# A cross-attention and FFN layer on one core: plain fp32 operands in place of pairs of fp32r parts in all FFN products

## The reference

```python
x = x + xattn(layernorm(x), ctx)       # 8 heads of 32, causal mask over 77 keys, softmax, projections Wq Wk Wv Wo with biases
x = x + ffn(layernorm(x))

def ffn(x):                            # weights are ternary (-1, 0, 1); s is a scale per output feature
    h = silu((x @ w1.T) * w1_s) * ((x @ w2.T) * w2_s)      # 256 -> 1024
    h = gelu((h @ h1.T) * h1_s)                            # 1024 -> 1024
    h = gelu((h @ h2.T) * h2_s)                            # 1024 -> 1024
    return (h @ w3.T) * w3_s                               # 1024 -> 256
```

## Time and profile before

| | |
|---|---|
| median of the runs | 1544.83 us |
| the profiled execution, its own time | 1543.65 us |
| its span, first to last instruction | 1541.9 us |
| PE (TensorE matmul) busy | 1532.9 us, 99% of the span |
| PEld (weight loads, beside PE) busy | 1249.0 us, 81% |
| DVE (VectorE) busy | 802.0 us, 52% |
| ACT (ScalarE) busy | 697.2 us, 45% |
| POOL (GpSimd) busy | 123.1 us, 8% |
| period of one pass of the loop | 92.78 us |

### The profile page before, as it was taken

One profiled execution on the slowest core, in us unless ns is written; L12 is line 12 of the kernel. 1 busy time (PEld: TensorE's weight loads), 2 busy tenths in 40 slices (PEclk: granted clock), 3 DMA queues, 4 the chain that ended last, 5 costly groups with the idle time before them and its releaser, 6 DMA issues.

```text
span 1541.9 us, 21318 instructions
## 1 busy us (share of the span) xinstructions
PE 1532.9 (99%) x8422; PEld 1249.0 (81%) x8422; DVE 802.0 (52%) x1276; ACT 697.2 (45%) x1013; POOL 123.1 (8%) x134
## 2 busy tenths in 40 slices
PE   9999999999999999999999999999999999999998
PEld 6787888888888887888888888887888888888887
DVE  6664735547354474644548354474644547354332
ACT  4653534436354453534536354353634536354342
POOL 1001011010100201001010100201001010100000
PEclk9999999999999999999999999999999999999999
DMA  9951020212202121020212202121030211202000
GB/s 377 347 189 50 32 84 27 75 48 65 57 14 77 53 67 49 31 85 27 75 41 64 65 14 75 55 67 49 24 92 27 75 41 64 64 16 68 14 1 15
DMA packets 50529, 106.32 MB, mean 69 GB/s; under 512 B 9026, under 2 KB 24394, under 8 KB 47690
## 3 DMA queue, kind: packets, MB, share of 16 engines
q1 hardware_dynamic: 50506, 106.00, 21.1%
HBM read 61.93 MB, written 32.52 MB: 61 GB/s over the span
## 4 chain that ended last, share of the span: by engine, by line
PE 96%; DMA 1%; SPq 1%; DVE 0%; ACT 0%; issue 0%; ACTq 0%
PE ffn_banks L479 84%; PE att_banks L660 4%; PE att_banks L602 3%; PE att_banks L619 2%; PE att_banks L650 2%; DMA h_bits<-in_h 1%; PE att_banks L670 1%; SPq L370 1%; PE ffn_banks L693 0%; ACT junk L725 0%; SPq L349 0%; PE ffn_banks L685 0%; DVE inexact L861 0%; PE att_banks L590 0%; DVE a_lo L887 0%
## 5 line engine op out<-in xcount | busy, mean ns | idle before, releaser
L479 PE MATMUL ffn_banks<-b_hi,h_sb 128*128 128x512 f32 x1024 | 404.4, 395 | 0.0
L479 PE MATMUL ffn_banks<-b_lo,h_sb 128*128 128x512 f32 x1024 | 399.0, 390 | 0.0
L479 PE MATMUL ffn_banks<-a_hi,h_sb 128*128 128x512 f32 x1024 | 398.3, 389 | 0.0
L479 PE MATMUL ffn_banks<-a_lo,h_sb 128*128 128x512 f32 x1024 | 398.3, 389 | 0.0
L759 ACT ACTIVATE a_f<-ffn_banks,vec 128x512 f32<-128x512 f32 x128 | 88.2, 689 | 367.1 <-PE ffn_banks L479 367.1
L887 DVE TENSOR_TENSOR a_lo<-a_f,a_hi 128x512 fp32r<-128x512 f32 x128 | 94.5, 739 | 298.0 <-ACT a_hi L760 297.9
L479 PEld LDWEIGHTS ffn_banks<-b_hi,h_sb 128*128 128x128 f32 x1024 | 192.3, 188 | 45.1 <-issue 6.2
L479 PEld LDWEIGHTS ffn_banks<-a_hi,h_sb 128*128 128x128 f32 x1024 | 192.2, 188 | 39.9
L479 PEld LDWEIGHTS ffn_banks<-a_lo,h_sb 128*128 128x128 f32 x1024 | 192.2, 188 | 39.9
L479 PEld LDWEIGHTS ffn_banks<-b_lo,h_sb 128*128 128x128 f32 x1024 | 192.3, 188 | 38.9
L479 PE MATMUL ffn_banks<-ln_hi,w_sb 128*128 128x512 f32 x512 | 203.6, 398 | 0.6 <-DVE v_later L915 0.6
(11 more groups left out here) (103 smaller groups left out, 1580.9 us busy)
## 6 DMA issues: line engine op xcount, KB each, us to landing
blocks_dram<-blocks SPq DMA_DIRECT2D x30, 512.0 KB, 3.0
attn_t<-blocks_dram SPq DMA_DIRECT2D x60, 256.0 KB
h_bits<-in_h SPq DMA_DIRECT2D x8, 1024.0 KB, 19.1
h_sb<-h_bits SPq DMA_DIRECT2D x8, 1024.0 KB, 8.5
out<-out_sb SPq DMA_DIRECT2D x32, 256.0 KB, 2.0
x_in<-in_x SPq DMA_DIRECT2D x15, 512.0 KB, 3.6
ln_t<-in_x_t SPq DMA_DIRECT2D x14, 512.0 KB, 4.4
ln_rows<-ln_rows_dram SPq DMA_DIRECT2D x14, 512.0 KB, 4.0
```

Source lines behind the costliest of these rows:

```text
L479: mm = nc.tensor.matmul(psum, left, right, start=(k == 0 and part == 0), stop=(k == rows - 1 and part == 1))
```

## The change

- The FFN's weights and hidden rows are plain fp32 tiles. Each FFN product is one matmul instruction in the program; `product`, `product_general`, `signal` and the parts `hi` and `lo` are gone, and with them the casts, the second Gelu and the subtractions, and the step `L1E`.
- The steps `CHECK`, `COUNT`, `FLAG`, `READ` and `KEEP`, the copies of the weights onto themselves, the ring, the general program and the branch are gone. TensorE waits for the loaded pieces themselves.
- From tile 1 on, the normalised rows are not transposed on TensorE: VectorE transposes 32x32 blocks (two instructions of 128x512), one DMA (`XW`) writes 512 KB to DRAM and four DMAs (`XR`) read them back into `ln2_t`. The tokens of a tile stand in another order in `ln2_t`; the Gelu of L3 puts them back. `T2` stays for tile 0.
- `PV` stands ahead of `L2` 7 instead of behind it, `O` behind `L3` 0 instead of `L3` 1, `LN1S` ahead of `LN2A`. SyncE's waits in `MV` and `ROWS` are other ones; buffers lie elsewhere, with their own room for `q_t`, `ln2_t` and `attn_t`.

```diff
-    ("L2", 1), ("MV", 0), ("L2", 2), ("MV", 1), ("L2", 3), ("L2", 4), ("L2", 5), ("L2", 6), ("L2", 7), ("PV", 0), ("PV", 1),
-    ("L3", 0), ("L3", 1), ("O", 0), ("CTX", 0), ("LN2S", 0), ("L3", 2), ("LN2A", 0), ("LN1S", 0), ("L3", 3), ("ROWS", 0), ("L3", 4),
-    ("L3", 5), ("LN1A", 0), ("L3", 6), ("T2", 0), ("L3", 7), ("Q", 0), ("L4", 0),
+    ("L2", 3), ("L2", 4), ("L2", 5), ("L2", 6), ("PV", 0), ("PV", 1), ("L2", 7),
+    ("L3", 0), ("O", 0), ("CTX", 0), ("LN2S", 0), ("L3", 1), ("LN1S", 0), ("LN2A", 0), ("XW", 0), ("ROWS", 0), ("XR", 0),
+    ("L3", 2), ("L3", 3), ("L3", 4), ("LN1A", 0), ("L3", 5), ("L3", 6), ("L3", 7), ("Q", 0), ("L4", 0), ("L4", 1),
...
-    ("KEEP", 0, 0), ("SPILL", 0, 0), ("KEEP", 1, 0), ("SPILL", 1, 0), ("KEEP", 2, 0),
+    ("SPILL", 0, 0), ("SPILL", 1, 0),
...
-                        if n == 0:
-                            sp.wait_ge(up_ready, KH * f + KH)
-                        else:
-                            sp.wait_ge(stored, 32 * f + 32)
+                        sp.wait_ge(stored, 32 * f + 32)
...
+                    if step == "XW":
+                        sp.wait_ge(rows_blocked, t)
+                        sp.dma_start(row_blocks_dram.rearrange("k p b i -> p k (b i)"), row_blocks[:].rearrange("p k b i -> p k (b i)"))\
+                            .then_inc(row_blocks_out, 16)
+                    if step == "XR":
+                        sp.wait_ge(row_blocks_out, 16 * t)
+                        sp.wait_ge(up_ready, KH * f + KH)
+                        for b_ in range(4):
+                            src = row_blocks_dram[:, :, b_, :].rearrange("k (r f) i -> f (k r) i", r=4)
+                            dst = ln2_t[32 * b_:32 * b_ + 32].rearrange("f k (r i) -> f (k r) i", r=4)
+                            sp.dma_start(dst, src).then_inc(ln2_there, 16)
...
-                    for part, x_ap in enumerate((hi(k), lo(k))):
-                        left, right = (x_ap, w_sb(k)) if w_is_moving else (w_sb(k), x_ap)
-                        mm = nc.tensor.matmul(psum, left, right, start=(k == 0 and part == 0),
-                                              stop=(k == rows - 1 and part == 1))
...
+                            for k in range(KD):
+                                mm = nc.tensor.matmul(fb[:, 2 * (n % 2) + i, :], w_sb[:, k, n * P:(n + 1) * P], ln2_t[:, k, :],
+                                                      start=(k == 0), stop=(k == KD - 1))
+                            mm.then_inc(ready, 1)
...
+                        for k in range(KH):
+                            if n == 0:
+                                pe.wait_ge(piece_loaded[first_piece + k // 2], 16)
+                            if n == 0 and (k == 0 or k >= at_once):
+                                pe.wait_ge(rows_done, KH * f + max(k + 1, at_once))
+                            mm = nc.tensor.matmul(fb[:, n % 4, :], w_sb[:, k, n * P:(n + 1) * P], rows[:, k, :],
+                                                  start=(k == 0), stop=(k == KH - 1))
...
+                                mm = nc.tensor.matmul(fb[:, 2 + n, i * D:(i + 1) * D], a_sb[:, k, j * P:(j + 1) * P], w3_sb[:, k, :],
+                                                      start=(k == 0), stop=(k == KH - 1))
...
-                        nc.scalar.activation(f32[:, n, :], fb[:, n % 4, :], ACT.Gelu, scale=scale[:, n:n + 1])
-                        nc.scalar.activation(hi[:, n, :], fb[:, n % 4, :], ACT.Gelu, scale=scale[:, n:n + 1]).then_inc(done, 1)
+                        if step == "L2":
+                            dst, src = rows[:, n, :], fb[:, n % 4, :]
+                        else:
+                            dst = rows[:, n, :].rearrange("p (j r q) -> p r j q", j=NQ, r=4)
+                            src = fb[:, n % 4, :].rearrange("p (r j q) -> p r j q", j=NQ, r=4)
+                        nc.scalar.activation(dst, src, ACT.Gelu, scale=scale[:, n:n + 1]).then_inc(done, 1)
...
+                            for k in range(KD):
+                                op = nc.vector.transpose(row_blocks[:, k, :, :],
+                                                         xln[:, :, k * P:(k + 1) * P].rearrange("p j (b f) -> p b j f", b=4))
+                            op.then_inc(rows_blocked, 1)
```

More of the change, by code:

```diff
@@ L141, in build_kernel @@
[L141 to L162, removed]
@@ L167, in build_kernel @@
+        put("later_rest", [P, 512])
+        c_later, _ = put("c_later", [P, KD * LATER], at=later_at)
+        v_later, _ = put("v_later", [P, NCH, D], at=later_at + 4 * KD * LATER)
+        assert later_at + 4 * KD * LATER + 4 * NCH * D <= top[0]
+        k_later, k_later_at = put("k_later", [P, HG * LATER])
+        q_t, _ = put("q_t", [P, HG, TILE])
+        ln2_t, _ = put("ln2_t", [P, KD, TILE])
+        attn_t, _ = put("attn_t", [TK, H, TQ])
         w_att_sb, _ = put("w_att_sb", [P, 4, KD, D])
@@ L295, in later_keys @@
             return k_later[:, HG * GROUP * g:HG * (GROUP * g + group_width(g))].rearrange("p (m n) -> p m n", m=HG)
[L297 to L314, removed]
         block = es.enter_context(nc.Block())
@@ L370, in load_piece, with one_pass @@
                 sp.dma_start(pieces[c][1], pieces[c][0]).then_inc(piece_loaded[c], 16)
[L372 to L390 removed]
+            def one_pass(f, a, b):
+                for step, n, t in steps(f, a, b):
                     if step == "SPILL" and n == 0:
@@ L471, in _ @@
         def _(pe):
-            def product(psum, w_sb, rows, hi, lo, ready, base_n, w_is_moving=False):
-                for k in range(rows):
-                    if ready is not None:
-                        pe.wait_ge(ready, base_n + k + 1)
-                    for part, x_ap in enumerate((hi(k), lo(k))):
-                        left, right = (x_ap, w_sb(k)) if w_is_moving else (w_sb(k), x_ap)
-                        mm = nc.tensor.matmul(psum, left, right, start=(k == 0 and part == 0),
-                                              stop=(k == rows - 1 and part == 1))
-                return mm
-            def product_general(psum, c, f, rows, hi, lo, ready, base_n, w_is_moving=False):
-                for k in range(rows):
-                    if ready is not None:
-                        pe.wait_ge(ready, base_n + k + 1)
-                    pe.wait_ge(ring_loaded[(c + k) % 2], (16 * (CHUNKS // 2)) * f + 16 * ((c + k) // 2 + 1))
-                    for part, x_ap in enumerate((hi(k).bitcast(F32), lo(k).bitcast(F32))):
-                        w_ap = ring[(c + k) % 2][:]
-                        left, right = (x_ap, w_ap) if w_is_moving else (w_ap, x_ap)
-                        mm = nc.tensor.matmul(psum, left, right, start=(k == 0 and part == 0),
-                                              stop=(k == rows - 1 and part == 1))
-                    mm.then_inc(ring_used, 1)
-                return mm
-            def signal(sem_, general):
-                if general:
-                    nc.tensor.drain().then_inc(sem_, 1)
             def spin(count):
@@ L565, in one_pass @@
-                        if general:
-                            signal(l4_ready, general)
-                        else:
-                            mm.then_inc(l4_ready, 1)
+                            for k in range(KH):
+                                if j == 0 and (k == 0 or k == KH - 1):
+                                    pe.wait_ge(gelu3_done, KH * f + max(k + 1, KH - 1))
+                                mm = nc.tensor.matmul(fb[:, 2 + n, i * D:(i + 1) * D], a_sb[:, k, j * P:(j + 1) * P], w3_sb[:, k, :],
+                                                      start=(k == 0), stop=(k == KH - 1))
@@ L663, in one_pass @@
                         mm.then_inc(o_ready, 1)
-                    if step == "T2":
+                    if step == "T2" and f is None:
                         pe.wait_ge(ln_ready[1], t + 1)
-                        if f is None:
-                            pe.wait_ge(q_done, 2)
+                        pe.wait_ge(q_done, 2)
                         for k in range(KD):
@@ L968, in one_pass @@
                         ln_apply(x1, 1, t)
-                    if step == "T2":
-                        dve.wait_ge(ln2hi_done, t + 1)
-                        nc.vector.tensor_tensor(ln2_lo[:], ab[:, 0:2, :], ln2_hi[:].bitcast(F32), ALU.subtract).then_inc(ln2t_done, 1)
+                        if f is not None:
+                            dve.wait_ge(ln_ready[1], t + 1)
+                            for k in range(KD):
+                                op = nc.vector.transpose(row_blocks[:, k, :, :],
+                                                         xln[:, :, k * P:(k + 1) * P].rearrange("p j (b f) -> p b j f", b=4))
+                            op.then_inc(rows_blocked, 1)
                     if step == "LN1S":
```

224 lines of the change are left out of this document (56 added, 168 removed), and 18 rows, old and new, of tables (FIRST, ORDER).

## The result

The changed kernel takes 2662.14 us (median of four runs, 2661.05 to 2663.31) against 1544.57 us: a ratio of 1.7234, 95% interval 1.7204 to 1.7264. The profiled execution has a span of 2659.3 us with a mean granted clock of 1.000, 1117.4 us longer than before.

The account below looks back on a forecast made before the run. TensorE bounds the kernel by what its matmuls cost back to back; 1541.9 + 1130 (FFN products) - 13 (transposes) - 3 (beginning) - 1 (a wait) = 2655 us of span, 2658 us in time, range 2635 to 2700.

Parts of the forecast that it names:

- the likeliest case: Whole kernel: the forecast itself, 2658 us, with its own range 2640 to 2675 us and chance 0.86.
- What bounds the kernel: TensorE's matmuls back to back set the time; shortening another engine's work cannot show.
- The products of L1 to L3: FFN layers L1 to L3: 320 records a tile go from 0.2267 to 0.4283 us each, adding 64.5 us a tile.
- anything but 428 ns: Sign of being wrong: plain records in L2 following one another at any distance other than 428 ns.
- L4: Last FFN layer, 256 columns: 64 records a tile go from 7.70 to 13.8 us, adding 6.1 us a tile.
- rival B: FFN's plain records carry the fp32r stream's surcharge of 13.4 ns: 72 us more, 2730 us; chance 0.06.
- rival A: L1 to L3: a long plain stream runs quicker, a product costing what a pair costs; 1528 us; chance 0.02.
- T2 and the way through DRAM: Transposes leave TensorE for tiles 1 to 15: 13 us less, the DRAM way of about 30 us hidden under 65 us.
- rival C, D: C: DRAM way exceeds its 65 us cover, 2733 us, chance 0.04. D: clock partly at 1.2 GHz, 2.9 ms, 0.02.
- ScalarE's and VectorE's relief: Casts, second Gelus and subtractions removed: some 280 us less busy time each, no gain in the kernel's time.
- The beginning: Before the loop: between 0 and 6 us can go, 3 us taken; first L1 at 62 to 67 us.

Follow-up runs that it names:

- e1_l3_plain: Kernel before with plain fp32 operands in L3 only, without its low-part subtraction and the second Gelu ahead of it; span 1956.1 us, time 1957.88 us.
- e2_t2_on_pe: Changed kernel with the normalised rows' transposes back on TensorE for every tile, no way through DRAM; span 2672.8 us, time 2674.63 us.
- e5_plain_halves: Changed kernel with each 512-column product of L1 to L3 issued as two of 256 columns; span 2672.4 us.
- e10_parts_dram_early: Kernel before with rows through DRAM, in the changed kernel's order around O and the layer norms, split into parts behind Q; 1531.09 us, ratio 0.9906.
- e3_parts_dram: Kernel before, fp32r parts kept, with normalised rows of tiles 1 to 15 transposed on VectorE and brought through DRAM; 1545.60 us, ratio 0.9999.
- e4_hi_only: Kernel before with the low parts' FFN matmuls left out, the work that makes them kept; span 1337.4 us.
- e7_late_rows: Changed kernel with the normalised rows' DRAM write and reads moved from L3 1 to behind L4 0 and its store; span 2750.0 us.
- e8_start_order: Changed kernel with the keys' and values' products before the loop back in the old kernel's places; span 2656.6 us.
- e9_grouped: Kernel before with each FFN sum's high parts all issued first, then all low parts; span 1560.0 us.
- e6_parts_halves: Kernel before with each 512-column part in L1 to L3 issued as two of 256 columns; span 1620.9 us.

## Why the prediction was right

It was right: 2658 us forecast, 2662.14 measured, inside the range of 2635 to 2700 and inside the likeliest case's own. By its steps:

- **What bounds the kernel.** Right: the chain after is TensorE's, and the experiments that changed TensorE's records moved the span by their price as long as TensorE stayed the bound (`e1_l3_plain`, `e2_t2_on_pe`, `e5_plain_halves`, `e10_parts_dram_early`; not `e3_parts_dram` and `e4_hi_only`, where another chain took over).
- **The products of L1 to L3.** 64.5 us a tile forecast, 64.6 measured. Q's short stretch spoke for the long one: 428.3 ns read there, 429.2 in the FFN. Over 5120 records the 0.9 ns are 4.6 us, mostly offset by smaller extras at the switches between steps (0.6 us a pass against 0.8), which I had held constant; that the two sums agree to 0.1 us is in part luck. Taken to the letter, my sign of being wrong ("anything but 428 ns") was drawn too narrowly. The row that foretold the pace was the one of the same kind of operand in another step, not the one of the FFN itself.
- **L4.** 6.1 us a tile forecast and measured, 215.8 ns a record against 215.6.
- **The surcharge (rival B) and the quicker stream (rival A).** Neither came: plain records keep 2.5 ns beyond their columns in long streams and in halves, parts 13 ns in both. The trace's 429.2 ns for two walks over 512 columns agrees with the columns over 2.4 GHz plus 2.5 ns that the Trainium skill gives for an isolated matmul ("TensorE: Matmul & The Clock Gate", section "Back-to-back issue gap"), taken for 1024 columns; the 226.7 ns of a part do not agree with it, being 10.9 ns above its value for 512. That section's 131 ns for 512 columns in a stream is seen in no run here, neither with plain operands nor with parts.
- **T2 and the way through DRAM.** 13 us forecast, 13.5 by `e2_t2_on_pe`. From O's end to the last reads I allowed 30 us; it took 18 (O's end at 328.4, the last reads landed at about 346.7), and `e7_late_rows` shows 7.5 us from the write's issue to L1. The argument had a gap that did not matter in the changed kernel: I followed the chain that was moved and left out the one behind it on VectorE, the next tile's statistics, which the transposes on TensorE had covered, and what the new traffic may do to that chain's DMA steps. `e3_parts_dram` shows that it takes the whole gain in the short pass. I had also priced a lost cover at 15 us for each us; with the clock it is 15 x 6.0 for 3.6 us of waiting, 1.7 times that (rival C, D).
- **ScalarE's and VectorE's relief.** Worth nothing, as forecast. The amounts were 241 and 259 us and not 280. The weight loads' share fell to 50% and not to 47%.
- **The beginning.** Wrong by 3.5 us: I took 3 us off the 67.8 us and it became 68.2, outside the 62 to 67 us that I had named. I had checked what the removed checks gave and not where the value products went; `e8_start_order` gives 2.65 us back, and with it the forecast of the span, 2655 us, would have been met to 2 us.

## What to carry to other kernels

On TensorE price a change of operand kind by the distance of starts of the same kind of record elsewhere in the trace, counting records for a product: here plain fp32 has two of two walks each, a pair of fp32r parts two of one walk, so with one operand exact in one part the pair was 1.9 times faster at 512 columns (453 against 858 ns) and 1.8 times at 256 (241 against 432 ns), as long as the work of making the parts stayed hidden under TensorE. Work on other engines saved in exchange is worth nothing under such a bound. When work leaves the bounding engine, look for the chain that it was covering and for transfers that will now run beside that chain's own: nearly the same edit took 12 us off the span in one order of steps and nothing in another.

## What the runs showed of the hardware

- A record of fp32r costs 13 ns beyond its columns at 2.4 GHz, at 512 columns (226.7 ns) and at 256 (119.9); a record of plain fp32 2.5 ns beyond two walks over its columns (429.2 and 215.8). The cause of the difference was not found. It does not hang on whether the record before had the same weights (`e9_grouped`), and the length of a weight load does not set the pace: the loads show 188 to 192 ns each and follow one another 120 ns apart in `e6_parts_halves`. Whether an fp32r load adds something fixed is open, since every record has a load.
- In `e7_late_rows` a wait of 3.6 us ahead of L1 was followed by 5.3 us with a mean granted clock of 0.69, between the lower level of 1.2 GHz and the upper; the eight records behind it took 5.27 us in this pass and 6.57 in another, in place of 3.43. In `e3_parts_dram`, with waits of up to 1.7 us, the mean granted clock is 1.000, and 1.00 in the 4.2 us around the wait shown. The page's row of 40 slices can't tell the two apart, since it has nines throughout in both; the mean (0.986 in `e7_late_rows`) and short windows can.
